# One step of the mixer's state scan: products in one operation, decay on ScalarE, update as one subtraction

## The reference

```python
def step(state, rkv):
    r_t, k_t, v_t = rkv
    pred = jnp.einsum('bhij,bhj->bhi', state, k_t)
    err = pred - v_t
    state = dec * state - et * (err[..., :, None] * k_t[..., None, :])
    n = jnp.maximum(jnp.sqrt(jnp.sum(state * state, axis=(-2, -1), keepdims=True)), 1e-08)
    state = state * jnp.where(n > max_norm, max_norm / n, 1.0)
    wkv = jnp.einsum('bhij,bhj->bhi', state, r_t)
    return (state, wkv)
...
state, wkv = jax.lax.scan(step, state0, (rs, ks_, vs))
```

## Time and profile before

| | us |
|---|---|
| median of 3 runs | 8376.84 |
| lowest, highest | 8373.83, 8382.36 |
| the profiled execution | 8381.71 |
| its span (first to last instruction) | 8379.6 |
| the mixer's scan in it, about | 1095 |
| VectorE busy over the span | 6666.1 |

### The profile page before, as it was taken

One profiled execution on the slowest core, in us unless ns is written; L12 is line 12 of the kernel. 1 busy time (PEld: TensorE's weight loads), 2 busy tenths in 40 slices (PEclk: granted clock), 3 DMA queues, 4 the chain that ended last, 5 costly groups with the idle time before them and its releaser, 6 DMA issues. The chain is left out here.

```text
span 8379.6 us, 122772 instructions
## 1 busy us (share of the span) xinstructions
PE 6244.1 (75%) x40740; PEld 4178.7 (50%) x40740; DVE 6666.1 (80%) x11381; ACT 3461.7 (41%) x6666; POOL 3671.7 (44%) x1911
## 2 busy tenths in 40 slices
PE   5455554888866677777777777777677769999999
PEld 3355554677755322222222222222244448888888
DVE  6799997555567899999999999999744547676765
ACT  3333332333323566666666566666444321212121
POOL 0000000111100599999999999999611112222222
PEclk8777776999988899999999999999888879999999
DMA  2211112111022100000000000000011110000000
GB/s 63 72 42 42 42 44 61 39 36 36 19 78 108 63 14 15 15 14 15 15 14 21 19 17 14 15 15 8 29 41 36 36 66 7 8 7 8 7 8 6
DMA packets 335677, 254.47 MB, mean 30 GB/s; under 512 B 161763, under 2 KB 307046, under 8 KB 334854
## 3 DMA queue, kind: packets, MB, share of 16 engines
q1 hardware_dynamic: 332774, 248.29, 9.5%
q10 hardware_dynamic: 2464, 0.26, 0.0%
HBM read 140.46 MB, written 108.00 MB: 30 GB/s over the span
## 5 line engine op out<-in xcount | busy, mean ns | idle before, releaser
L1809 POOL TENSOR_TENSOR ss_inp<-ss_dx,ss_b_all 128x1024 f32<-128x1024 f32 x1024 | 2390.2, 2359 | 230.1 <-ACT ss_b_all L1783 227.9
L1827 DVE TENSOR_TENSOR_SCAN ss_h<-banks,ss_inp 128x1024 f32<-128x1024 f32 x1024 | 2313.0, 2278 | 59.9 <-ACT banks L1775 59.9
L1747 PE MATMUL banks<-ss_ch,ident 128*128 128x512 f32 x4096 | 1959.5, 601 | 64.9 <-DVE ss_xc L1843 64.9
L1775 ACT ACTIVATE banks<-ss_dt,ss_neg_a 128x510 f32<-128x510 f32 x2048 | 1334.7, 688 | 2.7 <-DVE ss_h L1827 2.7
L1725 PE MATMUL banks<-ss_bc,ss_pick 96*128 96x512 bf16 x2048 | 747.0, 386 | 787.8 <-DVE ss_ch L1836 750.2
L1783 ACT COPY ss_b_all<-banks 128x512 f32<-128x512 f32 x1024 | 600.4, 586 | 1235.7 <-PE banks L1725 1232.0
L1747 PEld LDWEIGHTS banks<-ss_ch,ident 128*128 128x128 f32 x4096 | 788.0, 193 | 635.9 <-issue 577.9
L1725 PEld LDWEIGHTS banks<-ss_bc,ss_pick 96*128 (+1 forms) x2048 | 200.0, 98 | 1662.7 <-issue 1484.6
L1836 DVE TENSOR_TENSOR ss_ch<-ss_h,banks 128x1024 f32<-128x1024 f32 x768 | 917.9, 1195 | 0.0
L605 PE MATMUL banks<-ms_rprod,ident 128*128 128x128 f32 x2048 | 466.8, 400 | 507.9 <-DVE ms_rprod L691 507.9
L2139 POOL TENSOR_TENSOR pk_blockhot<-pk_onehot,pk_parts 128x2048 bf16<-128x2048 bf16 x96 | 345.5, 3628 | 1099.7 <-DVE pk_parts L2377 1099.7
(11 more groups left out here) (293 smaller groups left out, 10344.9 us busy)
## 6 DMA issues: line engine op xcount, KB each, us to landing
keep_v<-ms_cx_values SPq DMA_DIRECT2D x32, 512.0 KB, 2.8
l_va<-keep_v SPq DMA_DIRECT2D x32, 512.0 KB, 5.3
l_kf<-keep_k SPq DMA_DIRECT2D x32, 256.0 KB, 4.1
keep_x<-l_x SPq DMA_DIRECT2D x32, 256.0 KB, 2.2
keep_xc<-si_xc SPq DMA_DIRECT2D x16, 512.0 KB, 3.0
keep_zs<-si_zs SPq DMA_DIRECT2D x16, 512.0 KB, 4.0
keep_dt<-si_acc SPq DMA_DIRECT2D x16, 512.0 KB, 2.6
keep_dx<-si_acc SPq DMA_DIRECT2D x16, 512.0 KB, 2.6
```

The costliest lines, as they stand in the source:

```text
L1747: m = T_.matmul(sums[j][:, :], chip.ident[:, :], ch[u][:, j, :], start=first, stop=False, skip_group_check=True)
L1775: last = A.activation(decay[u % 2][:, j, :, 1:T], inputs[i % 2][0][:, j, :, 1:T], ACT.Exp, scale=neg_a[:, i % 2 * HB + j, bass.ds(k * UN + ...
L1809: G_.tensor_tensor(inp[u][:, :, :], inputs[i % 2][1][:, :, :, :].rearrange("p j g t -> p j (g t)"), rep(b_all[u][:, :], 1, HB), ALU.mult). ...
L1827: V.tensor_tensor_scan(flat(h[u][:, :, :]), decay[u % 2].rearrange("p j g t -> p (j g t)"), flat(inp[u][:, :, :]), 0.0, ALU.mult, ALU.add) ...
```

## The change

In `mixer_scan` four things are different.

- k and r live in one tile, `KR`, in which r stands one token later than k. So the k of token t and the r of token t - 1 lie side by side, and one instruction multiplies the state with both (`multiply`, 1024 values). Its products are in `products`, in the two buffers of four that `rprod` had. Every product, and not each fourth, now raises the semaphore that TensorE waits for (`multiplied`).
- The reduction of the k-product comes right behind that instruction and waits for it. `inv` and `FF` come behind the reduction.
- `fdec` comes ahead of `pred` and wakes ScalarE (`factored`). ScalarE makes `decayed`, the old state times `fdec`, in two activations with a scale per partition.
- The new state is `decayed` minus `outer`, one subtraction of 512 values on VectorE, which waits for both of ScalarE's pieces (`decay_done`). ScalarE squares both halves behind it, as there is no signal for the first half any more.

```diff
-    K_, R_, VV = sb("K", [P, T, 2, D]), sb("R", [P, T, 2, D]), sb("VV", [P, T, 2, D])
+    KR, VV = sb("KR", [P, T + 1, 2, 2, D]), sb("VV", [P, T, 2, D])
...
+    def r_of(ps, c):
+
+        return KR[ps, c * CH + 1:(c + 1) * CH + 1, 1, :, :]
...
-                T_.wait_ge(*multiplied_r.at(q))
+                T_.wait_ge(*multiplied.at(t))
...
+            A.wait_ge(*factored.at(t))
             for e in range(2):
-                A.wait_ge(*(state if e else half).at(t))
+                A.activation(flat(decayed[:, e, :, :]), flat(S_[:, t % 2, e, :, :]), ACT.Copy, scale=fdec[:, e:e + 1]).then_inc(decay_done.sem, 1)
+            A.wait_ge(*state.at(t))
+            for e in range(2):
                 A.activation(square[:, :], flat(S_[:, (t + 1) % 2, e, :, :]), ACT.Square, accum_out=n2[:, e:e + 1]
...
-        m = V.tensor_tensor(rprod[:, n // GR % 2, n % GR, :, :].rearrange("p (e i) j -> p e i j", e=2), S_[:, t % 2, :, :, :],
-                            rep(R_[:, n, :, :], 2, D), ALU.mult)
-        if n % GR == GR - 1:
-            m.then_inc(multiplied_r.sem, 1)
+        both = slice(0 if t < T else 1, 2 if t else 1)
+        m = V.tensor_tensor(products[:, n // GR % 2, n % GR, both, :, :, :], rep(S_[:, t % 2, :, :, :], 1, both.stop - both.start),
+                            rep(KR[:, t, both, :, :], 3, D), ALU.mult)
+        return m
...
-        V.tensor_tensor(prod[:, :, :, :], now, rep(K_[:, t, :, :], 2, D), ALU.mult).then_inc(*own.up())
-        multiplied = own.now()
+        multiply(V, t).then_inc(multiplied.sem, 1)
+        V.wait_ge(*multiplied.at(t))
+        V.tensor_reduce(raw[:, :], products[:, (t - 1) // GR % 2, (t - 1) % GR, 0, :, :, :].rearrange("p e i j -> p (e i) j"), AX.X, ALU.add
+                        ).then_inc(*own.up())
         if t:
-            r_product(V, t)
             V.wait_ge(*rooted.at(t - 1))
             V.tensor_scalar(inv[:, :], root[:, :], 1.0 / max_norm, 1.0, ALU.mult, ALU.max).then_inc(*own.up())
-        inverted = own.now()
-        V.wait_ge(*multiplied)
-        V.tensor_reduce(raw[:, :], prod[:, :, :, :].rearrange("p e i j -> p (e i) j"), AX.X, ALU.add).then_inc(*own.up())
-        if t:
-            V.wait_ge(*inverted)
+            V.wait_ge(*own.now())
             V.reciprocal(FF[:, t, :], inv[:, :]).then_inc(*own.up())
         V.wait_ge(*own.now())
+        if t:
+            V.wait_ge(*decay_done.at(t - 1))
+        V.tensor_tensor(fdec[:, :], FF[:, t, :], dec[:, :], ALU.mult).then_inc(factored.sem, 1)
         V.tensor_tensor(by_e(pred[:, :]), by_e(raw[:, :]), rep(FF[:, t, :], 2, D), ALU.mult).then_inc(*own.up())
         predicted = own.now()
-        V.tensor_tensor(fdec[:, :], FF[:, t, :], dec[:, :], ALU.mult).then_inc(*own.up())
...
-        for e in range(2):
-            V.scalar_tensor_tensor(flat(after[:, e, :, :]), flat(now[:, e, :, :]), fdec[:, e:e + 1], flat(outer[:, e, :, :]),
-                                   ALU.mult, ALU.subtract).then_inc((state if e else half).sem, 1)
+        V.wait_ge(*decay_done.at(t))
+        V.tensor_tensor(after, decayed[:, :, :, :], outer[:, :, :, :], ALU.subtract).then_inc(state.sem, 1)
```

More of the change, by code:

```diff
@@ L533, in mixer_scan @@
     sb = st.sb
-    K_, R_, VV = sb("K", [P, T, 2, D]), sb("R", [P, T, 2, D]), sb("VV", [P, T, 2, D])
+    KR, VV = sb("KR", [P, T + 1, 2, 2, D]), sb("VV", [P, T, 2, D])
     WKV, FF = sb("WKV", [P, 2, CH, 2, D]), sb("FF", [P, T + 1, 2])
     S_ = sb("S", [P, 2, 2, D, D])
-    prod, outer = sb("prod", [P, 2, D, D]), sb("outer", [P, 2, D, D])
-    rprod = sb("rprod", [P, 2, GR, 2 * D, D])
+    outer, decayed = sb("outer", [P, 2, D, D]), sb("decayed", [P, 2, D, D])
+    products = sb("products", [P, 2, GR, 2, 2, D, D])
     square = sb("square", [P, D * D])
@@ L551, in mixer_scan @@
     own, eks = st.steps("vector"), st.mark("ek_ready")
-    half, state, rooted = st.mark("first_head_ready"), st.mark("state"), st.mark("rooted")
-    squared, multiplied_r, summed_r, cut = st.mark("squared", 2), st.mark("r_multiplied"), st.mark("r_summed"), st.mark("r_cut")
+    state, rooted, factored, decay_done = st.mark("state"), st.mark("rooted"), st.mark("factored"), st.mark("decay_done", 2)
+    squared, multiplied, summed_r, cut = st.mark("squared", 2), st.mark("multiplied"), st.mark("r_summed"), st.mark("r_cut")
     measured, spread_root, spread_ready = st.mark("measured"), st.mark("spread_root"), st.mark("spread_ready")
@@ L558, in tokens, with k_of, v_of @@
         return slice(c * CH, (c + 1) * CH)
+    def k_of(ps, c):
+        return KR[ps, tokens(c), 0, :, :]
+    def r_of(ps, c):
+        return KR[ps, c * CH + 1:(c + 1) * CH + 1, 1, :, :]
+    def v_of(ps, c):
+        return VV[ps, tokens(c), :, :]
     def load_steps(engine, c, name, dst):
         for b in range(B):
-            engine.dma_start(dst[b * HP:(b + 1) * HP, tokens(c), :, :].rearrange("h t e d -> h t (e d)"),
+            engine.dma_start(dst(slice(b * HP, (b + 1) * HP), c).rearrange("h t e d -> h t (e d)"),
                              dr[name][b][tokens(c)].rearrange("t (h x) -> h t x", h=HP)).then_inc(steps[c % 2].sem, DMA)
     def sync(S):
-        load_steps(S, 0, "k", K_)
-        load_steps(S, 0, "v", VV)
+        load_steps(S, 0, "k", k_of)
+        load_steps(S, 0, "v", v_of)
         context.load_weights(S)
@@ L572, in sync @@
             if c + 1 < CHUNKS:
-                for name, dst in (("k", K_), ("v", VV), ("r", R_)):
+                for name, dst in (("k", k_of), ("v", v_of), ("r", r_of)):
                     load_steps(S, c + 1, name, dst)
@@ L602, in tensor @@
                 o = q * GR % CH * 2 * D
-                products = rprod[:, q % 2, :, :, :].rearrange("p t n j -> p (t n) j")
+                by_r = products[:, q % 2, :, 1, :, :, :].rearrange("p t e i j -> p t (e i) j")
                 for j in range(D):
-                    m = T_.matmul(bank[5 + q * GR // CH % 2][:, o:o + GR * 2 * D], chip.ident[:, :], products[:, :, j],
+                    m = T_.matmul(bank[5 + q * GR // CH % 2][:, o:o + GR * 2 * D], chip.ident[:, :], by_r[:, :, :, j],
                                   start=j == 0, stop=j == D - 1)
@@ L618, in scalar @@
                         ).then_inc(rates.sem, DMA)
-        load_steps(A, 0, "r", R_)
+        load_steps(A, 0, "r", r_of)
         A.wait_ge(*rates.at(0))
@@ L657, in vector @@
         V.wait_ge(*state.at(T - 1))
-        r_product(V, T)
+        multiply(V, T).then_inc(multiplied.sem, 1)
         V.wait_ge(*rooted.at(T - 1))
@@ L684, in measure, with multiply @@
             V.bn_stats(moments[:, e, c * 6:(c + 1) * 6], WKV[:, c % 2, :, e, :]).then_inc(*own.up())
-    def r_product(V, t):
+    def multiply(V, t):
         n = t - 1
@@ L704, in step @@
         c, u = t // CH, t % CH
-        now, after = S_[:, t % 2, :, :, :], S_[:, (t + 1) % 2, :, :, :]
+        after = S_[:, (t + 1) % 2, :, :, :]
         by_e = lambda a: a.rearrange("p (e i) -> p e i", e=2)
```

2 lines of the change are left out of this document (1 added, 1 removed).

## The result

| | before | with the change |
|---|---|---|
| median, us | 8377.05 (14 runs) | 8397.65 (14 runs) |
| lowest, highest | 8373.50, 8384.93 | 8391.69, 8400.92 |
| ratio to before | | 1.0023, 95% interval 1.0014 to 1.0031 |
| span of the profiled execution | 8379.6 | 8395.7 |

The change makes the kernel 20.6 us slower, with an interval of 12 to 26 us. The forecast was 17.3 us slower, and the time, 8397.65, lies in its range.

A forecast was written before the change was run, and what follows sets the result against it. VectorE's own order was taken to bound the 256 steps. The new step summed to 4.234 us against 4.160 read, taken as +0.07; over 254 steps 17.8, less 0.5, gave 8394 us, range 8380 to 8412.

The forecast's parts named there:

- The two spacings: On VectorE, an operation waiting for its predecessor starts 0.035 us after its end, otherwise 0.083 before; a wait costs 0.118.
- The state update: Two VectorE operations become one subtraction; S to the next product falls from 0.917 to 0.726 us, gain 0.19.
- The product and its wait: Joined 1024-element product, then the waiting reduction: 1.224 + 0.035 = 1.259 us against 1.29 before, gain 0.03 only.
- `inv` and `FF`: Both behind the reduction, one waiting for the other: 0.603 + 0.197 us against 0.596, loss 0.20.
- `fdec`: Ahead of `pred` on VectorE: `FF` to `fdec` 0.200 us, `fdec` to `pred` 0.077, against 0.19 before; loss 0.09.
- The size: The whole step was taken as 0.07 us longer; over 254 steps 17.8 us, +17.3 on the median.
- The two ends: First step's `inv` wait for the root and the last r-product: 0.5 us taken off the sum.
- The cover: ScalarE's scaled copies need 1.135 us from `fdec`'s start, VectorE needs them at 1.249: hidden with 0.11 us to spare.
- ScalarE ends last: Rival: the subtraction waits for the second scaled copy; 8403 or 8408 us, chance 0.12 for 8400 to 8415.
- The late context copy: One step in sixteen, ScalarE's copy waits for TensorE; 1.23 us falls to some 0.6, ending just in time.
- The rival by count of operations: At the two merges: operations count, waits don't; 0.424 us a step saved, 108 us, 8269 us; chance of faster 0.06.
- Waits cheaper: Rival: no 7 ns surcharge on new waits, wide product 1205 ns; +0.02 to +0.03 a step, 8382 to 8385; chance 0.12.

The follow-up runs named there:

- e4: The changed kernel without ScalarE's scaled copies, the new state being the old one undecayed minus the outer product; 8395.49 us.
- e3: The changed kernel, but the reduction sums the k-products of the token before, so it needn't wait for the product just ahead; 8366.67 us.
- e1: The kernel before with only the decay on ScalarE and one subtraction on VectorE; products, inv, FF, pred and fdec as before; 8386.32 us.
- e12: e6 with the context's copies one step later and the wait for ScalarE's pieces written ahead of the wait for outer; 8361.37 us.
- e6: The changed kernel with inv ahead of the reduction and a scratch tile for each of ScalarE's two squares; 8352.70 us.
- e2: The changed kernel with the old two-operation state update, the old squares, and fdec behind pred; 8422.92 us.
- e16: e15 with the products as in the kernel before: k-product, r-product, inv, then the reduction; 8345.54 us.
- e15: e12 with the two waits ahead of S back in the changed kernel's order, outer first and ScalarE's pieces second; 8342.89 us.
- e10: e1 with the two waits ahead of S swapped, ScalarE's pieces first, then VectorE's own outer product; 8377.89 us.

## Why the prediction was right

- **The bound.** VectorE's own order set the step before and after: S starts 0.03 to 0.04 behind `outer` in all 256 steps of both. e4 shows the other side: without ScalarE's copies the scan is 1103.9 instead of 1104.8.
- **The two spacings.** 0.035 behind the end with a wait, 0.083 ahead of it without. e3 changed nothing but that, and the 1.26 became 1.14.
- **The terms.** The state update: S to product was to be 0.726, and the rows have 1014.79 to 1015.52. The product and its wait: 1.259 reckoned, 1.26 read. `inv` and `FF`: 0.603 + 0.197, read 0.60 + 0.19. `fdec`: 0.200, read 0.20. The sum was 4.234, and the step is 4.23. The small surcharge of 7 ns after a wait was there: 679 became 686, and `FF` went from 155 to 166.
- **The size.** +0.07 a step was taken, and the scan shows 18.7 / 255 = 0.073. The 1 us by which that is more than 255 x 0.07 lies in the five odd steps, which the sum didn't have. The kernel as a whole lies 20.6 us higher; the 1.9 us between are within the interval, and nothing in the runs says what they are.
- **The two ends** were reckoned at 0.5 us, and gave back less. The first step went from 5.16 to 4.98, as the root now holds `inv` for 0.7 us instead of 0.9; behind the last S the first operation that waits for TensorE starts 8.89 instead of 9.08 us later. That is 0.18 + 0.19.
- **The cover was mis-sized.** 0.11 us was reckoned, with 0.035 for the way back from ScalarE. But the wait for ScalarE is written second, and costs 0.10 (e1, e12). So S could have started for ScalarE's sake at 1018.88 + 0.10 = 1018.98, and started at 1019.02: the real cover was 0.04. It held with less than half of what was reckoned, and no term of the prediction knew of the dearer wait; so far that was luck, and the rival "ScalarE ends last" was nearer than its price said.
- **The late context copy** was reckoned as just in time, with its wait for TensorE down from 1.23 to some 0.6 us. It is 0.6 (10.0 us in 16 chunks), and no wait of S shows in the changed kernel. In e3, where VectorE is 0.12 a step faster, it shows in 14 steps, in e6 in 16.
- **The rival by count of operations** fell in e2 (46 us slower, 38 faster forecast by it), in e3 and in e16. The rule of the Trainium skill (VectorE: DVE Perf Modes, "The DRAIN you can't avoid"), by which a semaphore behind each of eight chained copies costs nothing extra, doesn't carry over to these: the wait in e3 costs 0.12 us on operations of 1.22 and 0.69 us.
- **"Waits cheaper"** fell too: the joined product took the upper end of the earlier trace rows, 1225 ns.

What the sum could not say is which part was to blame, since it only added them. The joined products with `inv` behind the reduction cost 46 us alone (e2), and it is the order that costs: with `inv` ahead, the join is worth nothing or some 4 us gained (e15 against e16). The merge of the update alone costs 9 (e1), as ScalarE turns from hidden to last. Together they cost 21. Argued from the rows, and not tested apart: the longer products give ScalarE's root time enough, and `fdec` ahead of `pred` pays VectorE's time for ScalarE's.

## What to carry to other kernels

In a chain on one engine, count the places where an operation waits for the one just ahead as well as the operations; independent work between a producer and its reader is worth a wait each time, and a merge that takes it away can cost more than the instruction it saves. Before work is moved to another engine, sum its way there and back against what is left on the path; less than 0.1 us of cover is lost by moving one small operation, and a second wait on the instruction can take most of it. And put two edits into one run only when each has been seen alone.

## What was not expected of the hardware

- Where VectorE's instruction has two waits, the order in which they are written matters: 0.035 us from signal to start for the first, 0.10 for the second (e1 and e10, and e12 and e15, differ in that order alone). Over 255 steps it was 18.5 us between e12 and e15. The runs show it for the instruction that writes S and its two semaphores; why it is so, they don't say.
- This one is of the program, not of the chip: ScalarE's second square waited for the first only because both wrote one scratch tile. Two tiles let `inv` start 0.13 us earlier (e6), which gave 23 us in all.
